# First attention: the head attention's steps dealt at 0.6 a part of a step instead of 0.5, and a tile's output turned one tile later

## The chip, the cores and the metric

The kernel runs on one core of a Trainium2 chip. The metric is the device time of one execution in microseconds (us). The engines are TensorE (PE, with its weight loads PEld), VectorE (DVE), ScalarE (ACT), GpSimd (POOL) and SyncE (SP), whose queue issues most of the DMAs of the part looked at here.

## The reference, cut to what matters

```python
x = x + attn(cond(x, fside, mask, ..., cond_64, ...), ...)   # the part that changes
x = x + ffn(cond2(x, cond_64, ...), ...)                     # mixture of experts, attention, experts: unchanged

def cond(x, attn_bias, mask, ...):     # x: 8 x 512 x 256; 16 heads of 64, one key/value head
    xn = layernorm(x, g_in); q = xn @ Wq; k, v = split(xn @ Wkv)   # plus one null key and value
    sim = q @ k.T * scale + bias       # 512 x 513, causal and masked
    out = softmax(sim) @ v @ Wo
    return layernorm(out, g_out)

def attn(x, ...):                      # attention of each token over its own 16 heads of 16
    q = x @ Wq + bq;  k, v = split((x @ Wdown + bdown) @ Wup + bup)
    att = softmax(einsum('bthd,btgd->bthg', q, k) / 4)
    return einsum('bthg,btgd->bthd', att, v) @ Wout + bout
```

The rotary factors of the second attention cancel, since query and key of a token have the same position.

## The kernel before, in words

The program has five parts with a barrier (`meet`) between them. Part 0 is the first attention over the 8 sequences of the batch ("blocks", b); part 1 is the head attention of the last block together with the first routing of the experts; parts 2 to 4 are the rest. Only part 0 is touched.

**One order for all engines.** `order_one` writes a single list of entries such as `("score", b, p, t)`. Each engine's program (`tensor_one`, `vector_one`, `scalar_one`, `gpsimd_one`, `sync_one_steps`) walks through the same list in order and issues its own share of each entry, behind waits on semaphores. Whoever waits holds up all of its own later work.

**The main stream.** `step(m)` for m = 0 to 65 yields 12 parts. It works on three pairs of heads at once: scores (`score`, TensorE: matmuls L520 and L523; VectorE L672 adds the bias and finds the row's maximum; ScalarE L856 is the exponential in `soft`), the transposes of the pair before (`turn_p`, L534 and L867), and values, division and projection of the one before that (`values` L541, L548, L843; `divide` L684; `project` L558). `queries` (L509) prepares the next pair. Eight steps make a block. Scores use a ring of four PSUM banks, so the next scores wait for L672 of the ones before. When a block's last pair is through, in the steps 9, 17, 25 and so on, its output is normalised (`pn_turn` L689 and L567, `null` L573, `norm_o` L707 with a power on GpSimd, L924).

**The side streams.** Behind each part of a step every stream in `side` gets its rate added to a counter; when this reaches 1, one entry group of the stream goes into the list. `pre_steps` (rate 0.18, from step 9, 17, ...) normalises and turns the next block's input; its `norm_x` is four activations of ScalarE (L820). `head_steps(b)` (rate 0.5) is the head attention of the block whose normalisation has just been done. It begins at the steps 10, 18, 26, ..., 58; what the previous one still holds is put into the list there and then, in one go.

**head_steps.** It begins with `turn_h` twice (L581) and `lat` (L588). Then three things are woven for each of the four tiles of 128 tokens: `front` (`q2` L595, `kv2` L601; VectorE adds the bias L713, ScalarE copies L888 and L889), `middle`, 11 entries (`hs` 0 to 3: four products of GpSimd L784, each summed by VectorE L796 in the entry behind it; `hs_soft`: last sum, maximum L726, difference L728, exponential on ScalarE L894; `hs_sum`; `hv` 0 to 3: four products again; `hv_end`: last sum and the division L741), and `back` (`turn_o`: TensorE turns the tile's output L608, ScalarE copies it L899, SP loads the input rows, GpSimd adds a bias to them L935; one empty entry; `x1`: matmuls L616, VectorE's addition L746, SP's store). In round i the loop weaves `front` of tile i, `middle` of tile i - 1 and `back` of tile i - 2. That makes 52 entries. At 0.5 the second part of a block's first step gets the first of them, the 96 parts of the eight steps get 48, and 4 are left.

Products write to a ring of three buffers (`prod`), the tile's output goes to `ob` with two buffers, each free again when `turn_o` has read it; `xr` has two buffers too.

Of the kernel before, what the change touches and what calls it, by code (L numbers as in the profile page):

```python
# [17 lines left out]
NB = 8  # L18
S = 512
NT = 4  # L20
# [169 lines left out]
def weave(*streams):  # L190
    done = [0] * len(streams)
    total = max(n for _, n in streams)
    for k in range(1, total + 1):
        out = []
        for i, (g, n) in enumerate(streams):
            while done[i] < n * k // total:
                done[i] += 1
                out += next(g, [])
        yield out
    rest = [x for g, _ in streams for part in g for x in part]  # L200
    if rest:
        yield rest
# [28 lines left out]
def pre_steps(b):  # L231
    yield [("ln_x", b)]
    yield [("norm_x", b)]
    yield [("turn_x", b, 0)]
    yield [("turn_x", b, 1)]
    yield [("keys", b)]
    yield [("vals", b)]


def head_steps(b):  # L240
    yield [("turn_h", b, 0)]
    yield [("turn_h", b, 1)]
    yield [("lat", b)]

    def front(t):
        yield [("q2", b, t)]
        yield [("kv2", b, t)]

    def middle(t):
        for u in range(4):  # L250
            yield [("hs", b, t, u)]
        yield [("hs_soft", b, t)]
        yield [("hs_sum", b, t)]
        for u in range(4):
            yield [("hv", b, t, u)]
        yield [("hv_end", b, t)]

    def back(t):
        yield [("turn_o", b, t)]
        yield []  # L260
        yield [("x1", b, t)]

    for i in range(NT + 2):
        parts = []
        if i >= 2:
            parts.append((back(i - 2), 3))
        if i < NT:
            parts.append((front(i), 2))
        if 1 <= i <= NT:
            parts.append((middle(i - 1), 11))  # L270
        yield from weave(*parts)


def order_one():

    out = [("ln_x", 0), ("norm_x", 0), ("fold_key",), ("turn_x", 0, 0), ("turn_x", 0, 1), ("keys", 0), ("vals", 0),
           ("fold_value",), ("queries", 0, 0)]
    half = H // 2  # L280
    last = NB * half

    def step(m):
        new, old, done = m < last, 1 <= m <= last, 2 <= m <= last + 1
        n, o, d = [(x // half, x % half) for x in (m, m - 1, m - 2)]
        score = lambda t: [("score", *n, t)] if new else []
        soft = lambda t: [("soft", *n, t)] if new else []
        turn = lambda *lots: [("turn_p", o[0], 2 * o[1] + j, lot) for j, lot in lots] if old else []
        x = [("values", *d)] if done else []
        yield x + ([("causal", m)] if m < half else []) + score(0) + ([("divide", *d)] if done else [])  # L290
        yield turn((0, 0), (0, 1)) + ([("nulls", *n)] if new else []) + soft(0)
        yield ([("normal", *o)] if old else []) + ([("queries", (m + 1) // half, (m + 1) % half)] if m + 1 < last else [])
        yield score(1)
        yield turn((0, 2), (1, 0)) + soft(1) + ([("spread", *o)] if old else [])
        x = [("project", *d)] if done else []
        end = done and d[1] == half - 1
        yield x + ([("pn_turn", d[0])] if end else [])
        yield score(2)
        yield turn((1, 1), (1, 2)) + soft(2) + ([("null", d[0], 0)] if end else [])
        yield [("null", d[0], 1), ("norm_o", d[0], 0)] if end else []  # L300
        yield score(3) + ([("norm_o", d[0], 1)] if end else [])
        yield []
        yield soft(3)

    side, hd = [], None
    for m in range(last + 2):
        if m == half:
            out.append(("clear",))
        if m % half == 1 and m // half + 1 < NB:
            side.append([pre_steps(m // half + 1), 0.18, 0.0])  # L310
        if m >= half + 2 and (m - 2) % half == 0:
            if hd:
                out += [y for part in hd[0] for y in part]
            hd = [head_steps((m - 2) // half - 1), 0.5, 0.0]
            side.append(hd)
        for x in step(m):
            out += x
            for s in side:
                s[2] += s[1]
                while s[2] >= 1.0:  # L320
                    s[2] -= 1.0
                    out += next(s[0], [])
    out += [y for part in hd[0] for y in part]
    return out, [y for part in head_steps(NB - 1) for y in part]


def setup_one(k, nc, ins):
    k.split = (k.hi - 160000) // 32 * 32
    sb, top = Arena(nc, k.base, k.split), Arena(nc, k.split, k.hi)
    k.order1, k.tail1 = order_one()  # L330
    k.xin = sb("xin", [P, NT, D])
    k.gin = sb("w_gin", [P, 2])
# [2094 lines left out]
```

## Time and profile before

| | us |
|---|---|
| median of 3 runs (2769.91 to 2787.14) | 2782.77 |
| profiled execution, its own time | 2783.21 |
| its span | 2781.1 |
| TensorE / VectorE / ScalarE / GpSimd busy in the span | 2150.5 / 1568.9 / 1161.0 / 980.4 |
| the first attention, part 0, about | 0 to 1172 |
| of it with head attention beside it | 235 to 1172 |

Busy time counts instructions, not waits. A busy TensorE is not one at its peak, since matmuls are pipelined. The line numbers are those of the program, L672 is line 672.

### The profile page before, as it was taken

To read this page: it belongs to the slowest core of one execution; us is meant where nothing else is said; L and a number is where in the kernel's file an instruction comes from. 1 tells how busy PE (TensorE), PEld (TensorE's weight loads), DVE (VectorE), ACT (ScalarE), POOL (GpSimd) and SP (SyncE) were. 2 spreads that over 40 slices of the span, in tenths; PEclk is the share of its full clock that TensorE was granted. 3 is DMA by queue.
4 is the path that set the end of the run, shared out by engine and by line. 5 is a ranking of instruction groups with operands and counts; after the bars stand their busy time and mean duration, and the time that the engine had idled before them with its cause. 6 is when DMAs were issued, how large, how long until landed. Compare 5 with 4: busy or idle time off the path is not lost.

```text
span 2781.1 us, 32334 instructions
## 1 busy us (share of the span) xinstructions
PE 2150.5 (77%) x10624; PEld 1261.0 (45%) x10624; DVE 1568.9 (56%) x3389; ACT 1161.0 (42%) x2960; POOL 980.4 (35%) x751
## 2 busy tenths in 40 slices
PE   3999898989898989552859735887987799743996
PEld 1555554555554545321438623343543344321764
DVE  2347777776767676656513535566756678231335
ACT  1766565656565657221114300443443445520221
POOL 0106565656565555533260122222232221214005
PEclk9999999999998999766879856888988999976998
DMA  6600000000000000111145354636445642542214
GB/s 216 219 1 15 10 15 10 15 10 15 10 15 13 1 16 5 31 48 58 62 161 156 115 110 94 130 81 113 91 102 102 107 92 41 176 150 81 65 58 127
DMA packets 168589, 204.30 MB, mean 73 GB/s; under 512 B 20329, under 2 KB 132457, under 8 KB 168170
## 3 DMA queue, kind: packets, MB, share of 16 engines
q1 hardware_dynamic: 128690, 144.75, 21.1%
q10 hardware_dynamic: 30520, 32.32, 3.6%
q0 software_dynamic: 9216, 25.18, 3.0%
q8 instruction: 87, 1.43, 0.2%
q14 instruction: 76, 0.62, 0.1%
HBM read 122.10 MB, written 79.43 MB: 72 GB/s over the span
## 4 chain that ended last, share of the span: by engine, by line
PE 52%; DVE 15%; POOL 9%; DMA 9%; issue 6%; ACT 3%; SPq 2%; ACTq 2%; POOLq 0%; DVEq 0%
PE ps L548 4%; PE ps L523 4%; PE ps L1685 3%; PE ps L509 3%; PE ps L534 3%; PE ps L1676 3%; PE ps L1663 3%; PE ps L558 3%; DVE pb L672 3%; DMA m_x<-y_scratch 3%; POOL prod L784 3%; PE ps L2011 2%; PE ps L2019 2%; PE ps L1162 2%; SPq L1611 2%
## 5 line engine op out<-in xcount | busy, mean ns | idle before, releaser
L1808 ACT ACTIVATE m_pt<-ps 128x512 f32<-128x512 f32 x512 | 285.2, 599 | 307.3 <-PE ps L1676 299.0
L672 DVE CUSTOM_DVE_ANT_0 pb<-ps,bias,snl 128x128 f32<-128x128 f32 (+3 forms) x512 | 260.5, 546 | 267.2 <-PE ps L523 265.6
L784 POOL TENSOR_TENSOR prod<-qs,kvs 128x1024 f32<-128x1024 f32 x120 | 286.0, 2408 | 282.9 <-issue 142.3
L1743 DVE TENSOR_REDUCE m_mx<-ps 128x1 f32<-128x512 f32 x512 | 326.3, 681 | 83.8 <-PE ps L1663 82.0
L784 POOL TENSOR_TENSOR prod<-sc,kvs 128x1024 f32<-128x1024 f32 x120 | 279.2, 2352 | 171.4 <-ACT sc L894 154.8
L1663 PE MATMUL ps<-m_ks,m_qs 96*128 96x512 f32 x512 | 241.6, 489 | 118.6 <-DVE m_mx L1743 94.8
L856 ACT ACTIVATE pb<-pb,mst 128x129 f32<-128x129 f32 (+3 forms) x512 | 283.9, 560 | 76.9 <-DVE mst L672 74.9
L1676 PE MATMUL ps<-m_qs,m_ks 128*128 128x512 f32 x512 | 241.3, 486 | 12.1 <-ACT m_pt L1808 11.5
L867 ACT ACTIVATE ptb<-ps 128x512 f32<-128x512 f32 (+2 forms) x384 | 178.0, 490 | 146.8 <-PE ps L534 145.3
L1663 PEld LDWEIGHTS ps<-m_ks,m_qs 96*128 96x128 f32 x512 | 106.5, 210 | 256.2 <-DVE m_mx L1743 150.9
L523 PE MATMUL ps<-kz,qT 64*128 64x128 f32 (+3 forms) x1024 | 185.6, 441 | 0.0
L534 PE MATMUL ps<-ident,pb 128*128 128x128 f32 x1280 | 181.5, 280 | 4.9 <-ACT rsb L843 4.0
L534 PEld LDWEIGHTS ps<-ident,pb 128*128 128x128 f32 x1280 | 138.6, 141 | 67.4 <-issue 49.0
L796 DVE TENSOR_REDUCE sc<-prod 128x64 f32<-128x1024 f32 x128 | 153.2, 1213 | 21.8 <-POOL prod L784 21.5
L548 PE MATMUL ps<-ptb,vt 128*64 128x512 f32 (+3 forms) x1024 | 158.3, 452 | 1.1 <-ACT kvs L889 1.1
L796 DVE TENSOR_REDUCE ob<-prod 128x64 f32<-128x1024 f32 x128 | 153.1, 1211 | 8.4 <-POOL prod L784 8.2
L1685 PE MATMUL ps<-m_pt,m_va 128*32 128x512 f32 x1024 | 146.3, 654 | 0.0
L1676 PEld LDWEIGHTS ps<-m_qs,m_ks 128*128 128x128 f32 x512 | 102.0, 201 | 94.4 <-ACT m_pt L1808 78.6
L1842 POOL DMA_INDIRECT m_yg<-ye_scratch,e_pos x64 | 63.6, 994 | 175.9 <-DVE m_x L1731 162.8
L509 PE MATMUL ps<-xnT,w_wq 128*128 128x512 f32 x256 | 123.6, 606 | 1.8 <-DVE oTT L684 1.8
L558 PE MATMUL ps<-w_wo,oTT 128*128 128x256 f32 x512 | 121.2, 380 | 0.8 <-DVE oTT L684 0.8
L520 PE MATMUL ps<-mneg,mone 64*128 64x128 bf16 (+3 forms) x512 | 79.8, 308 | 43.3 <-DVE mst L672 42.6
(302 smaller groups left out, 3743.1 us busy)
## 6 DMA issues: line engine op xcount, KB each, us to landing
qk_scratch<-m_part SPq DMA_DIRECT2D x32, 512.0 KB, 2.8
m_qs<-qk_scratch SPq DMA_DIRECT2D x128, 128.0 KB, 4.3
m_ks<-qk_scratch SPq DMA_DIRECT2D x128, 128.0 KB, 6.3
xe_scratch<-ob SPq DMA_DIRECT2D x1, 9216.0 KB
e_xs<-xe_scratch SPq DMA_DIRECT2D x36, 256.0 KB, 2.9
ye_scratch<-e_ys SPq DMA_DIRECT2D x36, 256.0 KB, 2.1
hw_w<-in_w ACTq DMA_DIRECT2D x16, 512.0 KB, 3.9
xs_scratch<-ob SPq DMA_DIRECT2D x1, 4992.0 KB, 16.9
```

Source lines behind the costliest of these rows:

```text
L523: pe.matmul(ms[j].ap[:, 0:n], q.ap[DH * j:DH * j + DH, t * P:(t + 1) * P], kz.ap[DH * j:DH * j + DH, 0:n], start=False, stop=True, tile_po ...
L534: i = pe.transpose(m.ap[:, j * P:(j + 1) * P], pb[:, SEG[t] + kt * P:SEG[t] + (kt + 1) * P], ident[:, :])
L548: i = pe.matmul(m.ap[DH * j:DH * j + DH, kt * P:S], v.ap[:, kt, :], pt.ap[:, KEYCOL[kt]:KEYCOL[kt + 1]], start=(kt == 0), stop=(kt == NT - ...
L672: dv.tensor_tensor_reduce(pb.ap[:, j, SEG[t]:SEG[t] + n], rS.of(("S", b, p, t, j)).ap[:, 0:n], k.bias[:, h, CAUSAL[t]:CAUSAL[t + 1]], -1.0 ...
L784: e.tensor_tensor(out, one, two, ALU.mult).then_inc(*k.c.did(*product_done(step, b, t, u)))
L796: dv.tensor_reduce(heads(dst.ap[:, :])[:, 4 * u:4 * u + 4, :], src, AX, ALU.add).then_inc(*k.c.did(step + "_r", b, t, u))
L856: ac.activation(part, part, ACT.Exp, bias=ms[:, 0, j, t:t + 1], scale=-1.0, accum_out=ms[:, 1, j, t:t + 1]).then_inc(*did("exp", b, p, t, j))
L1663: pe.matmul(m.ap, k.qst[i][0:KM, h % 4, t * P:(t + 1) * P], k.kst[i][0:KM, h % 4, :], start=True, stop=True).then_inc(*did("m_S", b, h, t))
L1676: pe.matmul(m.ap, k.kst[i][:, j, kt * P:(kt + 1) * P], k.qst[i][:, j, :], start=True, stop=True).then_inc(*did("m_ST", b, g, kt, j))
L1685: i = pe.matmul(m.ap[32 * j:32 * j + 32, :], v.ap[:, kt, 4 * g + j, :], p.ap[:, j, :], start=(kt == 0), stop=(kt == NT - 1), tile_position ...
L1743: dv.tensor_reduce(x.ap[:, t, h:h + 1], k.qS.of((b, h, t)).ap, AX, ALU.max).then_inc(*did("m_max", b, h, t))
L1808: ac.activation(p.ap[:, j, :], k.qE.of((b, g, kt, j)).ap, ACT.Exp).then_inc(*did("m_exp", b, g, kt, j))
```

## The change

In `head_steps`, for all blocks but the last, `back` of tile i - 3 is woven instead of that of tile i - 2, and there is one round more: 55 entries instead of 52. In `order_one` the head stream's rate is 0.6 instead of 0.5. `head_steps` of the last block is not dealt in `order_one` and stays as it was. No instruction is added or removed.

```diff
@@ head_steps
-    for i in range(NT + 2):
+    late = 3 if b < NB - 1 else 2
+    for i in range(NT + late):
         parts = []
-        if i >= 2:
-            parts.append((back(i - 2), 3))
+        if i >= late:
+            parts.append((back(i - late), 3))
         if i < NT:
             parts.append((front(i), 2))
         if 1 <= i <= NT:
@@ order_one
             if hd:
                 out += [y for part in hd[0] for y in part]
-            hd = [head_steps((m - 2) // half - 1), 0.5, 0.0]
+            hd = [head_steps((m - 2) // half - 1), 0.6, 0.0]
             side.append(hd)
```

Counted from the part at which a block's stream begins (1 to 96), some entries stand in the list as follows:

| tile | `hs` 0, before / after | `hs_soft` | `hv` 0 | `kv2` of the next tile, `hv_end` | `turn_o` | `x1` |
|---|---|---|---|---|---|---|
| 0 | 12 / 11 | 20 / 17 | 24 / 21 | 32 / 27 | 40 / 52 | 54 / 64 |
| 1 | 34 / 29 | 42 / 36 | 46 / 39 | 54 / 46 | 62 / 71 | 76 / 82 |
| 2 | 56 / 47 | 64 / 54 | 68 / 57 | 76 / 64 | 84 / 84 | 96 / 87 |
| 3 | 78 / 66 | 86 / 72 | 90 / 76 | 96 / 82 | 96 / 89 | 96 / 92 |

## Rows read from the trace of the kernel before

**Rows 1.** The page's first line.
```profile
span 2781.1 us, 32334 instructions
```

**Rows 2.** Stages, steps 17 to 24: us, busy (instructions) of the engines, PEclk, DMA share, GB/s.
```profile
309.40:338.60 29.20, 18.92 (x100) 11.44 (x99) 21.55 (x58) 12.22 (x36) 13.39 (x11) 0.82 0.04 14
338.60:356.60 18.00, 17.81 (x104) 10.48 (x103) 5.20 (x20) 12.99 (x37) 4.00 (x2) 1.00 0.13 42
356.60:375.60 19.00, 18.55 (x119) 12.23 (x118) 13.65 (x33) 10.52 (x32) 12.25 (x6) 1.00 0.00 1
375.60:388.90 13.30, 13.30 (x82) 7.62 (x81) 10.83 (x25) 10.59 (x32) 6.42 (x3) 1.00 0.00 1
388.90:403.50 14.60, 13.03 (x82) 7.66 (x82) 11.25 (x30) 9.83 (x32) 11.90 (x7) 1.00 0.00 0
403.50:420.10 16.60, 14.02 (x85) 8.29 (x84) 13.07 (x26) 10.62 (x32) 12.53 (x7) 1.00 0.06 18
420.10:434.50 14.40, 13.60 (x84) 8.10 (x83) 11.01 (x30) 9.87 (x32) 8.48 (x5) 1.00 0.00 1
434.50:449.00 14.50, 14.05 (x85) 8.26 (x84) 13.28 (x26) 10.24 (x33) 11.31 (x6) 1.00 0.06 18
```

**Rows 3.** Waits of PE, 235 to 1148 us: us in total, times, longest.
```profile
PE ps L608 <- DVE ob L741: 60.1, 7, 9.2
```

**Rows 4.** Timeline at step 17's end: start, duration, instruction [idle before, releaser].
```profile
330.97 0.69 PE L608 MATMUL ps<-ident,ob 128*128 128x128 f32 x2 [9.19 <-DVE ob L741]
332.13 2.08 PE L616 MATMUL ps<-w_wout,oT 128*128 128x256 f32 x4 [0.47 <-ACT oT L899]
```

**Rows 5.** Timeline between the steps 9 and 10.
```profile
195.99 1.12 PE L534 MATMUL ps<-ident,pb 128*128 128x128 f32 x4 [2.82 <-ACT rsb L843]
```

**Rows 6.** Stages: a step without head work, steps 9, 10, and step 10's start.
```profile
153.40:166.10 12.70, 12.25 (x79) 7.10 (x78) 4.86 (x21) 9.56 (x30) 0.00 (x0) 1.00 0.00 0
178.70:196.00 17.30, 14.48 (x88) 8.52 (x86) 11.16 (x45) 11.61 (x34) 2.77 (x5) 0.98 0.00 0
196.00:217.00 21.00, 20.81 (x105) 12.30 (x106) 5.22 (x18) 13.03 (x37) 4.00 (x2) 0.86 0.11 35
...
196.00:201.00 5.00, 5.00 (x12) 2.76 (x12) 0.80 (x2) 2.63 (x9) 0.00 (x0) 0.50 0.01 3
```

**Rows 7.** Timeline of the steps 20 and 21.
```profile
394.90 1.22 DVE L796 TENSOR_REDUCE sc<-prod 128x64 f32<-128x1024 f32 x1 [1.57 <-POOL prod L784]
...
397.56 2.36 POOL L784 TENSOR_TENSOR prod<-sc,kvs 128x1024 f32<-128x1024 f32 x1 [2.69 <-ACT sc L894]
...
398.17 0.39 PE L520 MATMUL ps<-mneg,mone 64*128 64x512 bf16 x2 [1.57 <-DVE mst L672]
...
410.95 4.82 POOL L784 TENSOR_TENSOR prod<-qs,kvs 128x1024 f32<-128x1024 f32 x2 [4.07 <-ACT kvs L888]
411.16 2.41 DVE L741 TENSOR_TENSOR ob<-ob,sm 128x256 f32<-128x256 f32 x1
...
414.70 0.39 PE L520 MATMUL ps<-mneg,mone 64*128 64x512 bf16 x2 [2.58 <-DVE mst L672]
```

**Rows 8.** Groups, 309.4 to 449 us: busy us, mean ns | idle before, releasers.
```profile
L784 POOL TENSOR_TENSOR prod<-qs,kvs 128x1024 f32<-128x1024 f32 x17 | 40.1, 2384 | 32.2 <-issue 19.9 <-ACT kvs L888 12.3
L784 POOL TENSOR_TENSOR prod<-sc,kvs 128x1024 f32<-128x1024 f32 x16 | 37.3, 2354 | 19.9 <-ACT sc L894 17.7 <-DVE ob L796 2.2
...
L796 DVE TENSOR_REDUCE sc<-prod 128x64 f32<-128x1024 f32 x16 | 19.2, 1214 | 2.8 <-POOL prod L784 2.8
```

**Rows 9.** The line L741: shortest, median and longest ns, first and last start us.
```profile
L741 DVE TENSOR_TENSOR ob<-ob,sm x32: 424/427/6548, 244.5 to 1305.8; 128x256 f32<-128x256 f32 x32
```

**Rows 10.** Timeline of the last block of part 0.
```profile
1135.86 6.55 DVE L741 TENSOR_TENSOR ob<-ob,sm 128x256 f32<-128x256 f32 x1
...
1142.47 0.69 PE L608 MATMUL ps<-ident,ob 128*128 128x128 f32 x2 [5.57 <-DVE ob L741]
...
1172.01 0.42 DVE L746 TENSOR_TENSOR xr<-ps,xr 128x256 f32<-128x256 f32 x1 [3.33 <-PE ps L616]
```

## The prediction

> **What bounds the kernel now.** The profiled execution lasted 2783.2 us, of which the profile spans 2781.1 us [rows 1]; the median of the runs is 2782.8 us, so both stand for the same state. The change touches only the first attention, about 235 to 1172 us. I read that stretch with the view of stages, one window per step of the main order. Steps 17 to 24 make one period of the loop [rows 2]: it starts at 309.4 us, ends at 449.0 us and repeats in the same shape, 139.6 us each time. TensorE is busy 13 to 14 us of each ordinary step of about 14.7 us ((449.0 - 375.6) / 5), so it paces the ordinary steps. The exception is the first row of the period: 29.2 us for 18.9 us of matmuls. The view of waits says why: TensorE waited seven times, 60.1 us in all and 9.2 us at the longest, for the vector line L741, that is for `hv_end` [rows 3]. The timeline shows the place: the transposes of `turn_o` of the block's last tile start at 330.97 us after 9.19 us of idle time [rows 4]. It is the rest of the head stream, dealt in one burst at the end of the block.
>
> **Why the burst is there.** A step has 12 parts, a block of 8 steps has 96. At 0.5 a part the dealer hands out 48 of the 52 entries; the last four (`x1` 2 with `hv_end` 3, `turn_o` 3, an empty one, `x1` 3) come at once. `hv` 0 to 3 of that tile are dealt at parts 90 to 96, but GpSimd needs about 2.35 us for each product [rows 8], and TensorE reaches `turn_o` long before.
>
> **Part one, 0.6 a part.** The list grows to 55 entries; 0.6 x 96 = 57.6, so all are dealt, the last at part 92. `hv_end` 3 moves from part 96 to part 82 and `turn_o` 3 comes at part 89, so the 9.2 us wait goes. The clock goes with it: behind that stall the granted clock is low, and the four matmuls of `x1` take 2.08 us [rows 4], which would be about half at the full clock. An estimate: 1.0 us there and 0.8 us at the matmuls in front of and behind it, 1.8 us in all, so 11.0 us are the most a boundary can give back.
>
> **What lies under that stall.** The trace has a boundary without a burst: steps 9 and 10, where no head work had begun. They took 17.3 and 21.0 us [rows 6], against 29.2 and 18.0 us for steps 17 and 18 [rows 2]. Step 10 is 3 us longer than step 18 because ScalarE, busy with `norm_x`, delivers `rsb` late, TensorE idles 2.8 us [rows 5], and the clock granted in the next 5 us is 0.50, the lower level (1.2 GHz) [rows 6]. In the old kernel the burst stall hides this wait. So the new boundary pair is 17.3 + 21.0 + about 3.0 us for the matmuls of `x1` 2, `turn_o` 3 and `x1` 3 = 41.3 us, against 47.2. **Term one: -6.0 us a block.** Its bounds are -11.0 (nothing surfaces) and -3 (ScalarE and the normalisation wait longer than at step 9).
>
> **The price: the middle gets denser.** 11 entries a tile take 22 parts now and 18.3 parts then. At 1.22 us a part (14.7 / 12) that is 26.9 against 22.4 us. Three engines must fit:
> GpSimd: 4 x 2.38 + 4 x 2.35 = 18.9 us of products [rows 8], and between the two fours it waits at least 2.69 us for sum, maximum, difference and exponential at 397.56 us [rows 7]: 21.6 us, and the addition of the bias comes on top. It just fits.
> VectorE: a step without head work keeps it busy 4.86 us [rows 6], one with head work 10.8 to 13.3 us [rows 2]; the six from 356.6 to 449.0 us hold 73.1 us, less 6 x 4.86 leaves 43.9 us for 72 parts = 3.27 tiles, 13.4 us a tile. At 0.6 a step holds 4.9 + 13.4 x 12 / 18.3 = 13.7 us of 14.7.
> TensorE: the same matmuls, earlier.
> All instructions exist before and after; what is new is only where they wait for each other. Vector instructions are in order, so a `product_sum` that waits for GpSimd holds up the next masked maximum (L672), and its bank holds up the next scores on TensorE. The trace shows this chain at full rate: VectorE waits 1.57 us for a product, and TensorE then idles 1.57 us [rows 7]. In the old period such waits come to 2.8 us, two of them [rows 8]. In the new order `hs_soft` comes 6 or 7 parts behind `hs` 0 instead of 8, so the vector engine arrives 1.2 to 2.4 us earlier, while the four products take 9.5 us as before and start only when ScalarE has copied the result of `kv2`. Laid on the times of the old steps, I get waits of about 0 us for tile 0, 1.6 for tile 1 and 1.8 each for tiles 2 and 3: 5.2 us, less the 2.8 that exist. **Term two: +2.4 us a block**, bounds 0 and +5 (2 us for each of four tiles, less 2.8).
>
> **The port.** L741 takes 0.43 us in its median [rows 9] and 2.41 us where a product has just begun; TensorE then idles 2.58 us [rows 7]. This happens at two tiles a block, and the third could join, since GpSimd now has less idle time (4.07 us ahead of `hs` there). **Term three: +1.0 us a block**, half of one such wait, bounds 0 and +9 (below). The Trainium skill ("SBUF — State Buffer", section "Who interferes with whom") says that a vector instruction with two inputs in SBUF and a GpSimd instruction that reads SBUF exclude each other for the whole instruction. By that rule the longer form is one lock of at most a product's length, 2.4 us, and the sum would stay at 2764 us; by the longest row of this trace (rival B) it would be 2822. The trace agrees with the page where L741 ends right behind the first product.
>
> **The later output.** Turning tile t's output one round later removes no instruction. It keeps TensorE's `turn_o` 15 entries behind `hv_end` where 4 entries would now be only 6.7 parts. `ob` has two buffers; `turn_o` t is still dealt 4 entries ahead of the first `hv` sum of tile t+2. The DMA queue of SP carries one load and one store a tile as before; at the end of the block the load for tile 3 stands behind the store of `x1` 2, and GpSimd's addition of the bias waits for it, with the small powers of the normalisations queued behind. These are dealt 1 to 4 parts (1.2 to 5 us) later, which hides the load, so I cost it at nothing; without this cover `norm_o` and the next `turn_h` are late by up to 3 us, the bound -3 of term one. `late` stays 2 for the last block, whose tail is not changed.
>
> **The sum.** Six blocks (heads 0 to 5) x (-6.0 + 2.4 + 1.0 = -2.6) = -15.6 us. The seventh (head 6, steps 58 to 65) ends at the barrier: the last addition of `x1` starts at 1172.01 us [rows 10], behind the last products. With `hv_end` at part 82 a product, its sum and L741 (2.35 + 1.21 + 0.43 us) fall out of that last chain: -4 us, bounds 0 (the normalisation is as late) and -9 (four products). Total -19.6 us: 2783.2 - 19.6 = 2763.6 us, 0.7% faster.
>
> **Rivals.** A, TensorE paces everything and nothing new is exposed: -6.0 to -11.0 a block and -5 at the end, 2742 us, at best 2712 us. For it: GpSimd and VectorE both fit on paper. Against it: 1.57 us waits exist already at the slower deal. 0.27.
> B, the other side: the engines lock. At 1135.86 us, where GpSimd had begun the next tile while VectorE was still at the last sum, L741 took 6.55 us and TensorE idled 5.57 us instead of 2.58 [rows 10]. If this is the rule at three tiles a block, each costs 3.0 us more: -2.6 + 9 = +6.4 a block, +38 us, 2822 us. It decides as soon as GpSimd runs `hs` of the next tile before VectorE has done the fourth `hv` sum, so at a GpSimd lag of about 1.2 us. For it: GpSimd's chain of 21.6 us and more nearly fills its 22.4 us. Against: `kv2` is dealt with `hv_end`, which starts both together. 0.18. The Trainium skill's page just named speaks against it: there the lock ends with the instruction that holds it.
> C, the stall only moves: term two at its upper bound, so -6.0 + 5 + 1 = 0 a block, and -4 at the end: 2779 us. 0.12.
> The forecast: 0.43.
>
> **Range and chances.** About 1% (28 us) is what a measurement of this kernel tells from no change. Faster by more (under 2755): A and a fifth of the forecast, 0.35. Slower by more (over 2811): most of B, 0.16. Within: 0.49. The range 2735 to 2808 holds the forecast, C, the nearer part of A and of B; the forecast's own is 2748 to 2778.
>
> **What would show it.** Waits of TensorE for L741 near 0 before `turn_o`, and the first step of the period at 19 to 21 us instead of 29.2; the step behind it at 20 to 21 instead of 18.0 with a wait for `rsb`; ordinary steps at 15 to 16 us; vector waits for products above 2.8 us a period; L741's mean below 3 us. Wrong if ordinary steps stay under 14.8 us (then A) or L741 grows above 4 us (then B). Behind the barrier (1172 us in the old trace) nothing should change but the start.

## The result, and the profile after

| | before | after |
|---|---|---|
| median, us (runs, spread) | 2783.05 (4, 2769.91 to 2787.14) | 2756.61 (4, 2753.34 to 2762.67) |
| profiled execution, its own time / its span, us | 2783.21 / 2781.1 | 2759.01 / 2757.2 |
| ratio after / before, 95% interval | | 0.9913, 0.9888 to 0.9939 |

The kernel became 0.9% faster, 26 us by the medians; the forecast was 2763.6 us. The sum came out near, the terms did not: that is what the rest is about. In what follows "before" and "after" are the kernels before and after the change, and the numbers of one kernel's steps and waits are those of its one profiled execution. From L262 on the lines of the changed kernel are one higher (L672 is now L673, L741 is L742, and so on).

The stages of one period of after, steps 17 to 24, one window per step as in [rows 2] (us, then busy time and instructions of PE, PEld, DVE, ACT, POOL, the granted clock, DMA share, GB/s):

```profile
325.00:343.80 18.80, 16.80 (x98) 10.14 (x97) 12.07 (x48) 11.93 (x35) 3.51 (x6) 1.00 0.07 21
343.80:361.60 17.80, 17.80 (x105) 10.58 (x106) 6.34 (x19) 12.99 (x37) 4.17 (x2) 1.00 0.13 41
361.60:380.20 18.60, 18.49 (x118) 12.19 (x117) 14.53 (x34) 10.46 (x32) 14.27 (x7) 1.00 0.01 2
380.20:396.15 15.95, 13.88 (x82) 7.86 (x80) 12.72 (x29) 10.82 (x33) 9.98 (x6) 1.00 0.00 1
396.15:410.45 14.30, 13.73 (x81) 7.81 (x82) 11.86 (x25) 10.20 (x32) 12.17 (x6) 1.00 0.00 0
410.45:427.50 17.05, 14.93 (x84) 8.50 (x83) 12.18 (x29) 10.10 (x32) 14.36 (x8) 0.90 0.01 2
427.50:446.00 18.50, 14.13 (x84) 8.11 (x82) 16.25 (x31) 10.93 (x34) 12.41 (x7) 0.99 0.05 15
446.00:462.80 16.80, 15.29 (x85) 9.41 (x86) 10.54 (x25) 9.80 (x31) 9.54 (x5) 0.91 0.05 16
```

Read against [rows 2]: the first row fell from 29.2 to 18.8 us, the second stayed (18.0, 17.8). The next six grew from 92.4 to 101.2 us, most of all the one from 427.5 us on, 14.4 to 18.5. The sum fell from 139.6 to 137.8.

Waits of TensorE of after, 235 to 1148 us (us in total, times, longest), the view of [rows 3]:

```profile
PE ps L535 <- ACT rsb L844: 48.7, 19, 3.9
PE ps L521 <- DVE mst L673: 28.9, 36, 2.1
PE ps L549 <- DVE xr L747: 7.9, 7, 1.6
```

The 60.1 us for the division of `hv_end` are gone; a new first row of 48.7 us stands there: the transposes L535, which write to PSUM banks that ScalarE frees by its copies. The wait is named by `rsb` (L844), the ScalarE instruction ahead of them. The timeline shows the longest one, at the end of step 23, behind `hs_soft` of the block's last tile (part 72, the last of its step):

```profile
442.84 1.22 DVE L797 TENSOR_REDUCE sc<-prod 128x64 f32<-128x1024 f32 x1 [1.51 <-POOL prod L785]
444.10 0.42 DVE L727 TENSOR_REDUCE sm<-sc 128x16 f32<-128x256 f32 x1
444.55 0.42 DVE L729 TENSOR_TENSOR sc<-sc,sm 128x256 f32<-128x256 f32 x1
...
445.01 0.42 ACT L895 ACTIVATE sc<-sc 128x256 f32<-128x256 f32 x1 [3.68 <-DVE sc L729]
445.33 0.58 ACT L844 ACTIVATE rsb<-ps 128x512 f32<-128x512 f32 x1
...
445.97 1.11 PE L535 MATMUL ps<-ident,pb 128*128 128x128 f32 x4 [3.92 <-ACT rsb L844]
```

Four engines in a row. VectorE waits 1.51 us for GpSimd's fourth product. The last sum, the maximum and the difference follow on VectorE. ScalarE has stood 3.68 us at the exponential (L895), and `rsb`, ready to run behind it, stands there too. TensorE has then idled 3.92 us.

**Where the time went, part by part.** I take the start of each `divide` (L684, L685) as the start of a step.

- Start to step 10: 196.02 us before, 203.09 us after, though no entry differs up to there. Eight of the experiments below have the same order up to step 10; in seven of them it began at 195.4 to 199.5 us, in one (the earlier load) at 203.2 us. So these 7.1 us come and go with one order and are not the change's; their cause wasn't looked for.
- Steps 10 to 58, six blocks: 848.9 to 829.6 us, -19.3 us. The blocks gave 1.9, 2.0, 1.0, 2.2, 4.2 and 8.0 us. The last two are large because the old profile had single steps 1 to 3 us longer there than in its other blocks, and because step 57, where no `norm_x` stands any more, took 16.9 us in after instead of the 18.8 us of its other boundaries; the first four, 1.8 us on average, are the period itself.
- The last block, from the start of step 58 to the last store of part 0: 127.5 to 112.0 us, -15.5 us.
- Behind it: +1.8 us to the next part's first load, +2.1 us in all the rest (1606.8 and 1608.9 us).

The sum is 7.1 - 19.3 - 15.5 + 1.8 + 2.1 = -23.8 us, the difference of the spans (23.9) but for rounding.

The end of part 0 in after (timeline):

```profile
1137.25 0.43 DVE L742 TENSOR_TENSOR ob<-ob,sm 128x256 f32<-128x256 f32 x1
...
1144.69 0.33 SPq L462 DMA_DIRECT2D x_scratch<-xr  x1
```

and the same place before:

```profile
1158.58 0.71 POOL L924 TENSOR_TENSOR lnors<-lnove,mhalf 128x2 f32<-128x2 f32 x1 [4.88 <-DVE lnove L757]
...
1168.25 0.42 DVE L741 TENSOR_TENSOR ob<-ob,sm 128x256 f32<-128x256 f32 x1
...
1168.73 0.69 PE L608 MATMUL ps<-ident,ob 128*128 128x128 f32 x2 [7.74 <-DVE ob L741]
```

From the last `divide` to the last store it was 24.3 us before (1148.12 to 1172.46) and is 6.9 us now (1137.80 to 1144.69). The old tail ran the last sum of `hs`, the exponential, four products, four sums, L741, `turn_o` and `x1` in series, and GpSimd stood 4.88 us at the power of `norm_o` (L924) ahead of three of these products; now the products are through when the projection comes.

### The profile page after: what moved, and what is told of

Its sections match the earlier page's. It is cut to its first block, busy times and chain, and to the rows that moved or that the text cites. A ratio compares the mean times of both kernels' runs of the same rounds, so it can differ in the third digit from the quotient of the medians.

```text
span 2757.2 us, 32346 instructions
## 1 busy us (share of the span) xinstructions
PE 2156.8 (78%) x10624; PEld 1260.4 (46%) x10624; DVE 1540.5 (56%) x3389; ACT 1163.4 (42%) x2960; POOL 981.7 (36%) x751
## 4 chain that ended last, share of the span: by engine, by line
PE 51%; DVE 14%; POOL 12%; DMA 9%; issue 5%; ACT 3%; SPq 3%; ACTq 2%; POOLq 0%; DVEq 0%
POOL prod L785 6%; PE ps L510 4%; PE ps L1686 4%; PE ps L524 3%; PE ps L1677 3%; PE ps L1664 3%; PE ps L549 3%; PE ps L535 3%; DMA m_x<-y_scratch 3%; DVE pb L673 3%; DVE sc L797 3%; PE ps L559 3%; PE ps L2012 2%; PE ps L2020 2%; PE ps L1163 2%
## 5 line engine op out<-in xcount | busy, mean ns | idle before, releaser
L673 DVE CUSTOM_DVE_ANT_0 pb<-ps,bias,snl 128x128 f32<-128x128 f32 (+3 forms) x512 | 260.8, 547 | 254.4 <-PE ps L524 251.2
L535 PE MATMUL ps<-ident,pb 128*128 128x128 f32 x1280 | 187.5, 283 | 53.4 <-ACT rsb L844 52.7
L535 PEld LDWEIGHTS ps<-ident,pb 128*128 128x128 f32 x1280 | 142.3, 143 | 115.3 <-ACT rsb L844 57.9
L549 PE MATMUL ps<-ptb,vt 128*64 128x512 f32 (+3 forms) x1024 | 159.4, 455 | 7.9 <-DVE xr L747 7.9
L797 DVE TENSOR_REDUCE ob<-prod 128x64 f32<-128x1024 f32 x128 | 152.4, 1210 | 11.6 <-POOL prod L785 11.5
L510 PE MATMUL ps<-xnT,w_wq 128*128 128x512 f32 x256 | 132.9, 645 | 0.9
L549 PEld LDWEIGHTS ps<-ptb,vt 128*64 128x64 f32 x1024 | 71.4, 141 | 92.3 <-issue 81.6
## 6 DMA issues: line engine op xcount, KB each, us to landing
xs_scratch<-ob SPq DMA_DIRECT2D x1, 4992.0 KB, 16.9
```

What stands on the lines that cost most here:

```text
L535: i = pe.transpose(m.ap[:, j * P:(j + 1) * P], pb[:, SEG[t] + kt * P:SEG[t] + (kt + 1) * P], ident[:, :])
L549: i = pe.matmul(m.ap[DH * j:DH * j + DH, kt * P:S], v.ap[:, kt, :], pt.ap[:, KEYCOL[kt]:KEYCOL[kt + 1]], start=(kt == 0), stop=(kt == NT - ...
L673: dv.tensor_tensor_reduce(pb.ap[:, j, SEG[t]:SEG[t] + n], rS.of(("S", b, p, t, j)).ap[:, 0:n], k.bias[:, h, CAUSAL[t]:CAUSAL[t + 1]], -1.0 ...
L797: dv.tensor_reduce(heads(dst.ap[:, :])[:, 4 * u:4 * u + 4, :], src, AX, ALU.add).then_inc(*k.c.did(step + "_r", b, t, u))
```

## The experiments

Each period below is the mean distance of the division L742 of a block's last tile from block to block, over five blocks (before: 330.48 to 1036.68 us, 141.2, of which the first three are 139.6 to 139.9). A ratio is that of the medians of several runs; kernels whose intervals overlap are not told apart by it. A period is read from one profile, and a profile can lie off its kernel's median: the one of "0.6 alone, exponential later" is the fastest of ten runs (2774.5 us, median 2788.5), that of the last kernel the slowest of six (2721.7, median 2707.9). What lies behind part 0 took 1606 to 1633 us in these profiles, and differs as much between kernels that do the same there (1608.6 before, 1632.8 with the later output alone): a spread as large as the whole change. So the periods carry the argument about part 0.

| kernel | ratio, 95% interval | period, us |
|---|---|---|
| after | 0.9913, 0.9888 to 0.9939 | 138.2 |
| 0.6 alone | 1.0104, 1.0080 to 1.0128 | 146.8 |
| later output alone | 0.9952, 0.9934 to 0.9970 | 139.8 |
| 0.6, `turn_o` one entry later | 0.9932, 0.9906 to 0.9958 | 136.5 |
| 0.6 alone, exponential later | 1.0016, 0.9988 to 1.0045 | 143.2 |
| 0.55 alone | 0.9883, 0.9862 to 0.9905 | 135.7 |
| after, products halved | 0.9709, 0.9686 to 0.9732 | 133.1 |
| after, exponential later | 0.9857, 0.9795 to 0.9920 | 136.0 |
| after, load of `xr` earlier | 0.9907, 0.9873 to 0.9942 | as after |
| after, `norm_x` later | 0.9885, 0.9838 to 0.9933 | 138.2 |
| after, the last three together | 0.9759, 0.9699 to 0.9818 | 133.0 |
| the three, at 0.55 without the later output | 0.9710, 0.9674 to 0.9747 | 129.7 |

### The rate alone

```diff
-    late = 3 if b < NB - 1 else 2
+    late = 2
```

> The rate of 0.6 alone, with the output turned two rounds behind as before (52 entries, all dealt by part 87). My theory: the rate does all the work, since turn_o comes 6 to 7 parts (about 8 us) behind hv_end and TensorE does not catch up: ratio to before 0.990 to 0.993, waits of TensorE for L741/L742 under 5 us in all. Rival: the later output is needed, because TensorE runs into hv_end of tile 3 at part 82 (turn_o at part 84) and of other tiles: 2 to 5 us a block more, ratio 0.995 to 1.003.

Measured 1.0104: slower than the kernel before, and above both ranges. My theory that the rate does the whole work fell; the rival had the cause, and its price too small. The later output is worth 1.9% here, 8.6 us a block (146.8 less 138.2). TensorE's waits, 235 to 1148 us:

```profile
PE ps L535 <- ACT rsb L844: 51.9, 19, 3.9
...
PE ps L609 <- DVE ob L742: 19.3, 6, 3.2
```

The first row is nearly that of after (48.7); the other, 3.2 us a block, is new, and it is the old wait in a new place (timeline of step 24):

```profile
469.20 0.69 PE L609 MATMUL ps<-ident,ob 128*128 128x128 f32 x2 [3.21 <-DVE ob L742]
...
470.67 3.22 PE L549 MATMUL ps<-ptb,vt 128*64 128x512 f32 x16
```

`turn_o` 3 stands at part 84 there, `hv_end` 3 at part 82: TensorE is at the transposes before VectorE is at the division. And the clock: sixteen matmuls of L549 take 3.22 us behind that wait, 2.37 us in the same step of after. The stage from 453.40 us on, step 24, shows it:

```profile
453.40:475.05 21.65, 17.99 (x85) 10.01 (x86) 10.53 (x25) 10.02 (x31) 9.50 (x5) 0.80 0.04 12
```

Step 24 took 21.7 us against 16.8 in after, with the same 85 matmuls: 3.2 us of wait, and 17.99 instead of 15.29 us of busy time (granted clock 0.80, against 0.91). The other steps are 4 us longer in sum: steps 18, 19, 20 and 21 by 1.5, 1.6, 0.7 and 2.5 us, step 22 shorter by 1.7, step 25 by 0.6. At the boundary TensorE waits 2.8 us for `rsb` (2.0 in after), and step 18 behind it has a granted clock of 0.92 (1.00 in after).

### The later output alone

```diff
-            hd = [head_steps((m - 2) // half - 1), 0.6, 0.0]
+            hd = [head_steps((m - 2) // half - 1), 0.5, 0.0]
```

> The later output alone, at 0.5 a part: 55 entries, 48 dealt, 7 in the burst at the block's end (hv_end 3, turn_o 2, x1 2, turn_o 3, x1 3 among them). My theory: no gain, the wait for hv_end in the burst is shorter by the 1.5 to 3 us of matmuls that now stand in front of it but the two x1 follow each other through the same buffers: ratio 0.996 to 1.004, TensorE still waits 6 to 9 us a block for L741/L742. Rival: the later output itself frees TensorE, ratio below 0.995.

Measured 0.9952, between the two ranges. The burst at the block's end stays and has seven entries instead of four: step 17 took 31.6 us (29.2 before). Only the instruction that TensorE waits for has another name:

```profile
PE ps L617 <- DVE xr L747: 53.1, 12, 7.5
```

The period is that of the kernel before (139.8; 139.6 to 139.9 in the first three blocks of before). In its profile, where six blocks took 840.8 us (848.9 before, with the longer single steps named above), the last block is 4.2 us shorter: its last L742 came 116.4 us behind the start of step 58, against 123.3 before, without the 6.55 us division of [rows 10]. But the rest behind part 0 took 1632.8 us in that execution (1608.6 before), so the profile, at 2796.0 us, doesn't account for the ratio of the medians.

So neither half does what both do: +1.0% and -0.5% apart, -0.9% together. The halves interact, and the next run says where.

### `turn_o` one entry later

```diff
     def back(t):
-        yield [("turn_o", b, t)]
         yield []
+        yield [("turn_o", b, t)]
         yield [("x1", b, t)]
```

(with `late = 2` and 0.6: nothing but `turn_o` moves, from the parts 34, 52, 71, 84 to 41, 59, 77, 86)

> e1_rate_only with the empty entry ahead of turn_o instead of behind it: turn_o moves from the parts 34, 52, 71 and 84 to 41, 59, 77 and 86, x1 and all else stay where they are. If the loss of the rate without the later output comes from the place of turn_o (ahead of the next tile's hs_soft, and right behind hv_end at the last tile), TensorE's 3.2 us wait for L742 and the lower clock behind it go and the kernel comes to 0.992 to 0.998. If it comes from x1 and its vector addition L747 in the dense stretch, or from SP's load and store, it stays at 1.005 to 1.012.

Measured 0.9932, as the first theory expected; the period is 136.5 us instead of 146.8. In all blocks but the last the wait for L742 is gone (once, 4.2 us, remains in the last block):

```profile
PE ps L535 <- ACT rsb L844: 46.7, 19, 3.5
...
PE ps L609 <- DVE ob L742: 4.2, 1, 4.2
```

Step 24 took 14.1 us instead of 21.7. So the 1.9% that the later output is worth hang on the place of one entry, `turn_o`. A whole round isn't needed; for the last tile two parts were enough. The kernel isn't told apart from after by its ratio: its steps 20 to 24 are shorter in sum, and its boundary, steps 17 and 18, is longer (18.9 and 20.8 us against 18.8 and 17.9), with a wait of 2.84 us for `rsb` and a granted clock of 0.86 in step 18.

### The exponential later, without the later output

```diff
-        elif step == "hs_soft":
+        elif step == "hs_sum":
```

(in `scalar_one`, ahead of the exponential L895, with `late = 2` and 0.6)

> e1_rate_only (0.6, turn_o two rounds behind) with the exponential of hs_soft issued one entry later on ScalarE. If the 2% that this kernel loses against the full change come from ScalarE standing behind the exponential while oT and rsb are due (TensorE waited 51.9 us for rsb there), it comes back to 0.985 to 0.992. If they come from turn_o standing right behind hv_end (TensorE waits 3.2 us a block for L742 and the granted clock falls behind it), it stays at 1.000 to 1.010.

Measured 1.0016: the second theory's range. Both causes are in it, though: the waits for `rsb` fell and the period with them, 146.8 to 143.2 us, while the wait for L742 grew.

```profile
PE ps L609 <- DVE ob L742: 27.0, 6, 4.5
PE ps L535 <- ACT rsb L844: 14.4, 6, 2.8
```

### A rate between the two

```diff
-    late = 3 if b < NB - 1 else 2
+    late = 2
...
-            hd = [head_steps((m - 2) // half - 1), 0.6, 0.0]
+            hd = [head_steps((m - 2) // half - 1), 0.55, 0.0]
```

> Rate 0.55, output two rounds behind: all 52 entries are dealt by part 95, hs_soft falls at other parts (the last part of a step less often). If the density of the middle sets the price (8.8 us a block at 0.6), it is about half here, 4 us, and some 2 to 4 us of the wait at turn_o 3 come back: ratio 0.989 to 0.993. If the place of hs_soft inside a step sets the price (ScalarE's exponential in front of rsb), the price follows those places and not the rate: steps with hs_soft in parts 10 to 12 are 1.5 to 4 us longer, the others are not.

Measured 0.9883, a little below the range, with a shorter period than after (135.7 against 138.2 us). Against the same order at 0.6 (1.0104, 146.8 us) it is 2.2% faster. 0.55 x 96 = 52.8 entries, so all 52 are dealt and the burst is gone, as at 0.6; the middle is less dense:

```profile
PE ps L535 <- ACT rsb L844: 14.1, 11, 2.0
PE ps L521 <- DVE mst L673: 13.8, 34, 0.5
PE ps L542 <- ACT ptb L870: 12.8, 7, 1.9
PE ps L609 <- DVE ob L742: 9.2, 7, 2.1
PE ps L535 <- ACT pb L857: 7.3, 7, 1.1
```

14.1 us for `rsb` instead of 48.7, 13.8 for `mst` instead of 28.9; 12.8 and 7.3 us for other copies and exponentials of ScalarE are new. The 0.6 of the change paid for a burst that 0.55 removes as well. Part of what the blocks gain is lost at the end: six of them took 813.6 us (829.6 in after), but the last block, from step 58 to the last store, 121.4 us (112.0).

Which of the two theories holds isn't decided by this run. The steps 19 to 24 took 96.7 us, 4.3 more than before, as the density theory says. But the places changed with the rate: in after the two waits of 1.6 and 3.9 us stand where `hs_soft` falls on the last part of a step (parts 36 and 72), and at 0.55 it falls there at no tile (parts 19, 39, 59, 79, that is 7, 3, 11 and 7 of their steps). And ScalarE's standing at the exponential didn't fall: over the six blocks it is 80.2 us (after 60.8, before 41.9), for example 4.06 us in step 22 and 3.74 us in step 24. Other instructions are behind it there, and TensorE's waits for them are 1.0 and 1.1 us (step 22) and 1.9 us (step 24) instead of one of 3.9. So for these waits it counts what stands behind the exponential, and the place is the likelier cause; a rate with the same density and other places was not run.

### Products of half the size

```diff
-        out = pv.ap.rearrange("p (h g d) -> p h g d", h=4, g=H)
+        out = pv.ap[:, 0:512].rearrange("p (h g d) -> p h g d", h=2, g=H)
```

(and its operands, and the same for `hv`.) Each of GpSimd's products computes two of its four heads; the sums still run over the whole buffer. The head attention's result is not the reference's.

> The changed kernel, but each product of the head attention is computed for two of its four heads only (GpSimd about 1.2 us instead of 2.4; VectorE still sums the whole buffer, so its work is the same, and the sums are partly over old data). If the price in the middle is GpSimd's chain, the waits of VectorE for products (36 us) and of TensorE for rsb behind hs_soft (5.5 us a block) vanish and the steps 19 to 24 fall from 101.2 to 92 to 94 us: 45 to 60 us less in all, ratio to before 0.970 to 0.975. If VectorE's density is the price, the steps stay within 2 us of 101: ratio 0.988 to 0.992.

Measured 0.9709, in the range; the steps 19 to 24 were not: they took 95.8 us (20.0, 16.0, 14.3, 13.4, 16.9, 15.2) against 101.2 in after and 92.4 before; I had expected 92 to 94. The steps 17 and 18 stayed at 18.8 and 17.9 us. By steps, only part of the growth goes: step 20 keeps all of its 2.6 us over before, step 23 keeps 2.5 of 4.1, step 24 0.7 of 2.3. The largest gain, 3.7 us in this block, is in step 22, which had hardly grown; there the wait of 2.1 us for `mst` is gone and the granted clock is 1.00 instead of 0.90. (In after the steps 19 and 22 take 18.6 and 17.1 us in some blocks, 20.2 and 15.3 in others.) VectorE's waits for products went, as said (36.1 to 0.8 us). TensorE's first wait:

```profile
PE ps L535 <- ACT rsb L844: 37.3, 19, 2.3
```

With products of half the size TensorE still waits 19 times for `rsb`: 2.0 us at the boundary and 1.6 us in step 20 as in after, 2.3 us instead of 3.9 in step 23. In step 20 VectorE waits for no product in either kernel ahead of the last two sums, and ScalarE stands 2.08 us at the exponential in both. GpSimd alone isn't the cause: the order in VectorE's and ScalarE's queues is a second one.

### The exponential later, the load earlier, `norm_x` later

Three edits to after, one kernel each: the entry at which `scalar_one` issues the exponential L895, the one at which `sync_one_steps` loads `xr`, and the rate of `pre_steps`.

```diff
-        elif step == "hs_soft":
+        elif step == "hs_sum":
...
-        elif step == "turn_o":
+        elif step == "hv_end":
...
-            side.append([pre_steps(m // half + 1), 0.18, 0.0])
+            side.append([pre_steps(m // half + 1), 0.16, 0.0])
```

> The changed kernel with ScalarE's exponential of the head scores (L895) issued at the entry hs_sum instead of hs_soft, so behind values' copy rsb (L844) where hs_soft stands in the last part of a step. Theory ScalarE's queue: TensorE's waits of 1.6 and 3.9 us a block for rsb behind hs_soft go, that of 2.0 us at the block's end (norm_x) stays; 3 to 5 us a block less, ratio to before 0.979 to 0.985. Rival, VectorE's order: the same late difference holds up L673 as well, the wait comes back as one for mst or GpSimd's second four products start later: block time within 1 us of 137.8, ratio 0.988 to 0.994.

Measured 0.9857, with an interval that reaches into both ranges; the period fell by 2.2 us to 136.0, less than the 3 to 5 us of the theory. The exponential stands one entry later in ScalarE's program, so the copies that free TensorE's banks run in front of it. The waits moved as the theory says, but not all of them went:

```profile
PE ps L521 <- DVE mst L673: 40.7, 42, 2.1
PE ps L549 <- DVE xr L747: 16.8, 7, 2.7
...
PE ps L535 <- ACT rsb L844: 10.0, 5, 2.0
```

`rsb` fell from 48.7 to 10.0 us. 11.8 us came back as waits for the masked maximum (28.9 to 40.7) and 8.9 us as waits for L747 (7.9 to 16.8), both VectorE's. The wait at the boundary, 2.0 us for `norm_x`, stayed in its place, five times. But what follows it did not: step 18 took 19.5 us instead of 17.9. The first 5 us of step 18 in this kernel, then in after:

```profile
331.39:336.39 5.00, 5.00 (x18) 2.53 (x18) 0.80 (x2) 3.10 (x10) 0.00 (x0) 0.66 0.00 2
```

```profile
343.76:348.76 5.00, 5.00 (x33) 3.43 (x34) 1.70 (x6) 4.06 (x13) 0.00 (x0) 1.00 0.02 5
```

The step ahead took the same 18.8 us with 16.8 us of matmuls at 1.00 in both, and the wait was 2.00 us in both. So 1.7 us of what the edit gives are lost again in step 18 to the clock, for a reason that these profiles don't show.

> The changed kernel with SP's load of the input rows (L458) issued at hv_end instead of turn_o. It takes away GpSimd's waits for that load (85 us in all, 8.0 the longest). Theory: these waits cost little, since what stands behind them is not needed yet; only TensorE's wait for the addition L747 (7.9 us in all) goes: 1 us a block less, ratio 0.986 to 0.992. Rival: GpSimd's idle time there delays the normalisation and the next turn_h: 3 us a block or more less, ratio below 0.985.

Measured 0.9907, with the step times of after. GpSimd's waits for this load, 85.5 us in after, fell to 47.6 us, and its waits for VectorE at the two powers L917 and L925 grew instead (26.5 to 64.6 us). Nothing followed for the steps: its DMA wait lies beside time in which nobody needs it. TensorE's row L549 <- L747 stayed at 7.9 us, so it isn't the load that makes `x1` late.

> The changed kernel with pre_steps dealt at 0.16 instead of 0.18, so that norm_x stands behind rsb of the next step. Theory: the wait of 2.0 us for rsb at the block's end goes, 1.5 to 2.5 us a block, ratio 0.984 to 0.988. Rival: norm_x only moves the wait to another copy of the denser step 18, block time as before, ratio 0.989 to 0.994.

Measured 0.9885, just below the rival's range, with the period of after, 138.2 us, as the rival says. Step 17 got shorter by 1.7 us (17.1 instead of 18.8) and step 19 by 3.0 (15.6 instead of 18.6), but the steps 18 and 20 got longer by 1.0 and 3.4 us. `rsb` still has 19 waits, 40.8 us. Alone, the edit moves the wait of the boundary and doesn't remove it; what the median gained against after is within the intervals.

### All three, and all three at 0.55

> The three edits before together. If they act on different waits the gains add up: 5 to 8 us a block, ratio 0.970 to 0.980. If VectorE or GpSimd binds behind them, the gain stops near that of the best single one: 0.982 to 0.988.

Measured 0.9759, period 133.0 us. Of the waits for `rsb` 1.1 us are left; what part 0 still waits for is mostly VectorE's:

```profile
PE ps L521 <- DVE mst L673: 40.6, 42, 2.1
PE ps L549 <- DVE xr L747: 18.5, 7, 4.4
```

Its three edits took 2.2, nothing and nothing off the period alone, and 5.2 us together. Of the 3.0 us between the exponential's edit alone and all three, 1.9 us are step 18 (19.5 to 17.7 us): without the wait at the boundary the granted clock there is 1.00 again, not 0.91. In after there was no such loss behind the wait, so moving `norm_x` alone had less to win there. The load's share in the 3.0 us was not run apart.

> The three edits of e8_all (exponential issued behind the vector chain, xr loaded at hv_end, norm_x later) at a rate of 0.55 with the old output distance of two rounds. At 0.55 the middle of the block is less dense than at 0.6: the plain 0.55 kernel gave 0.988 with 14 us of TensorE waits for rsb. My theory (density of the vector chain costs about 5 us a block at 0.6, and the ScalarE queue what is left) expects 0.972 to 0.978, as good as e8_all. The rival (at 0.55 the ScalarE waits are mostly gone already, so the three edits have nothing to take) expects 0.984 to 0.989.

Measured 0.9710, 2707.9 us against 2783.2, a little below the range of the theory: the fastest kernel of the study that computes the reference's result, faster than before and after. The intervals of this ratio and of that at 0.6 (0.9759) overlap; the periods differ, 129.7 against 133.0 us. The last block gains nearly nothing here: 124.7 us from step 58 to the last store, 127.5 before. Its waits, then two blocks of it as a stage (its blocks take 128.5 and 130.5 us by turns):

```profile
PE ps L521 <- DVE mst L673: 16.5, 35, 2.6
...
PE ps L535 <- ACT rsb L844: 11.3, 14, 0.9
PE ps L609 <- DVE ob L742: 9.2, 7, 2.1
```

```profile
312.57:571.57 259.00, 246.93 (x1448) 147.49 (x1448) 193.33 (x464) 174.65 (x516) 160.63 (x82) 0.99 0.05 14
```

TensorE is busy 246.9 of 259.0 us, 95%. The same two blocks of after:

```profile
322.49:599.14 276.65, 251.12 (x1452) 149.44 (x1450) 193.05 (x465) 174.44 (x517) 160.82 (x82) 0.97 0.04 13
```

The 8.8 us a block between them are 6.7 us of idle time (12.8 to 6.0) and 2.1 us of TensorE's busy time, at a granted clock of 0.97 instead of 0.99. VectorE, ScalarE and GpSimd do the same work in the same busy time.

## Why the prediction was right, and where its steps were wrong

**The burst.** Right: the 9.2 us wait of [rows 3] is gone, step 17 takes 18.8 us (said 19 to 21).

**Term one, -6.0 a block, mis-sized.** It measured -10.6: the pair of steps 17 and 18 took 36.6 us (18.75 and 17.85) instead of 47.2, against the 41.3 that I took. I had let the wait of [rows 5] surface with its low clock behind it. It did surface, in step 17 and without the clock:

```profile
341.62 1.57 ACT L821 ACTIVATE xin<-xin,nmr,lnxrs 128x256 f32<-128x256 f32 x3
343.10 0.57 ACT L844 ACTIVATE rsb<-ps 128x512 f32<-128x512 f32 x1
...
343.73 0.66 PE L535 MATMUL ps<-ident,pb 128*128 128x128 f32 x4 [2.00 <-ACT rsb L844]
```

TensorE waited 2.0 us instead of 2.82, and the clock of step 18 stayed 1.00 (0.86 in step 10 of [rows 6]). "Step 18 at 20 to 21 us" was wrong for this kernel. The bound of -11 held the value; the choice within it was the pessimistic row. Why the clock stayed is open: with the exponential later the same wait of 2.00 us is followed by 0.91 in step 18 (19.5 us), and with `turn_o` one entry later a wait of 2.84 us by 0.86 and 20.8 us, as I had forecast. So part of the -10.6 is luck of this one order.

**Terms two and three, +3.4 a block, mis-sized the other way.** They measured +8.8 together, above the +5 that was the bound of term two. By steps 19 to 24, after less before: -0.4, +2.6, -0.2, +0.4, +4.1, +2.3 us. Two waits carry most of it: 1.6 us behind `hs_soft` of tile 1 (step 20) and 3.9 us behind that of tile 3 (step 23), with a granted clock of 0.91 in step 24 behind it.

The chain that I priced, a product holds VectorE and VectorE holds the masked maximum, is in the trace, but TensorE's waits for `mst` did not grow, 28.9 us after against this before:

```profile
PE ps L520 <- DVE mst L672: 37.5, 33, 2.6
```

The step that failed is the list of engines that must fit: it has GpSimd, VectorE and TensorE, not ScalarE. ScalarE is busy 11 us of a step, so it seemed to have room. But it takes its work in order, and the exponential of `hs_soft` waits for the end of the chain of the other two. At 0.6 `hs_soft` stands one or two parts nearer to the first product, so ScalarE stands at the exponential for longer (60.8 us over the six blocks, 41.9 before), with `rsb` and the copies behind it. The exponential moved (`rsb` 48.7 to 10.0 us) shows ScalarE's end of that chain; the products halved (the longest wait 3.9 to 2.3 us, that of step 20 unchanged) show that GpSimd is at its other end at tile 3 and not at tile 1. How long ScalarE stands is not the price by itself: at 0.55 it stands for 80.2 us and TensorE waits less. The price is what is queued behind the exponential, and in after that is `rsb` at both tiles whose `hs_soft` falls on the last part of a step. VectorE's waits for products, which I named as a sign, did grow: 36.1 us (31.4 and 4.7) from 235 to 1148 us, against 20.2 before in the same stretch.

**Term three, the third long L741.** Did not happen. The four divisions of a block took 0.42, 1.63, 2.42 and 0.42 us, against 0.43, 2.41, 2.42 and 0.42, and no TensorE wait names them in after.

**The later output.** I said what it keeps away, `turn_o` 4 entries (6.7 parts) behind `hv_end`, and gave it no price. At the last tile, where no other thread is woven in, it would be less: parts 82 and 84, and it is there that TensorE waits. The runs give the price: without it the same kernel is 1.9% slower. It stood in a sentence, not in the sum. The rest of that paragraph held: SP's queue and the load cost nothing (the earlier load changed no step).

**The last block, -4, mis-sized.** It measured -15.5, beyond the bound of -9. I took out one product, its sum and the division, at most four products. But the tail of [rows 10] was longer than its last entries: the exponential, all four products, the sums and the burst behind them ran in series, with 4.88 us of GpSimd's standing at `norm_o` among them (24.3 us against 6.9). The 6.55 us division is gone as well.

**The sum.** Six blocks gave -19.3 for a predicted -15.6, of which the period itself is 1.8 a block against the predicted 2.6, and the rest is what the old profile lost in single steps. With the last block, part 0 gave -34.8 instead of -19.6. The profile shows 7.1 us less of it because of its start and 3.9 us less behind the barrier. That the total came near the forecast is luck: term one was off by 4.6 us a block and the price of the middle by 5.4 the other way, the last block by 11.5 us, and a start that isn't the change's took 7.1 us back.

**The rivals.** A, nothing new exposed: no, though its term one was the right one; a TensorE that paces is seen only in the last kernel of the study. B, the long division at three tiles: no. C, term two at +5 and term one at -6: its direction in the middle was right and too small. The time lay between A's 2742 and the forecast.

## What to carry to other kernels

When entries of a side stream are dealt faster, list for each engine not its busy time but the instruction in its queue that waits for the end of the longest chain, and what stands behind that instruction: a ScalarE that was busy 63% of the time (87.2 of 138.3 us a block) held TensorE by its order. Try the smallest rate that still deals everything first (0.55, not 0.6, here), but look too at which part of a step the waiting instruction falls on: the rate moves that as well, and a wait of the same length costs more or less by what stands behind it. Place each consumer by its distance to its producer: moving one entry by two to seven parts was worth 1.7%. An edit that gives nothing alone (`norm_x` later) can give some 3 us a block (136.0 to 133.0, with the load) beside another one, so try the survivors together.

## What the runs showed of the hardware

**A short wait costs more than itself.** In the kernel with the rate alone a wait of 3.2 us was followed by step 24's 85 matmuls at 17.99 us busy instead of the 15.29 us of after, which hasn't that wait: 2.7 us more, at a granted clock of 0.80 over the step. The clock has two levels, 2.4 and 1.2 GHz; four matmuls L542 behind the wait took 1.06 us, which took 0.60 us at the full clock, so they ran near the lower one.

**The same wait, with and without the clock's fall.** The wait of 2.8 us at the end of step 9 stands in before, in after and in the kernel with halved products, with the same order ahead of it; the granted clock in the 5 us behind it was 0.50, 0.66 and 1.00, and step 10 took 21.0, 19.5 and 17.9 us. The wait of 2.0 us at the end of step 17 was followed by 1.00 in after and by 0.66 with the exponential later. So what a short wait costs in clock can't be read off its length, and a gain or loss of 2 to 3 us behind one is not yet the edit's.

**A division that waits for one product, or for three.** In after one L742 began 1.0 us behind the start of three products in a row and ended 0.25 us behind the end of the first (7.20 us for three, so 2.40 us each and the first over at about 409.50):

```profile
407.10 7.20 POOL L785 TENSOR_TENSOR prod<-qs,kvs 128x1024 f32<-128x1024 f32 x3 [2.13 <-ACT kvs L889]
...
408.12 1.63 DVE L742 TENSOR_TENSOR ob<-ob,sm 128x256 f32<-128x256 f32 x1
```

That is what the Trainium skill says ("SBUF — State Buffer", section "Who interferes with whom"): an exclusive hold for the whole instruction. But in the kernel with `turn_o` one entry later, and before in [rows 10], it ended only with the third product of three in a row:

```profile
1095.48 6.99 POOL L785 TENSOR_TENSOR prod<-qs,kvs 128x1024 f32<-128x1024 f32 x3
...
1097.00 5.75 DVE L742 TENSOR_TENSOR ob<-ob,sm 128x256 f32<-128x256 f32 x1
```

1097.00 + 5.75 = 1102.75 us, just behind the end of the third product (1102.47), though the first was over at about 1097.8. There the measurement differs from the page. Both times VectorE came to the division 1.3 to 1.5 us into the run of three, and GpSimd had come into that run straight from two other products; in the short case it had been idle for 2.13 us before it. Whether that decides between one product and three wasn't tried; in the blocks before the last it never happened.
